# Attention in a fused block: the maximum subtracted on GpSimd, one exponential per four heads, probabilities as the stationary operand

## What is computed

```python
x = x + tanh(g_xattn[0]) * experts8(layernorm(x), gates from ctx)   # 8 experts, 2 of them used
x = x + tanh(g_ffn[0])   * swiglu4(layernorm(x), own router)        # 4 experts, 2 of them used
x = x + tanh(g_xattn[1]) * attention(layernorm(x), ctx, ctx, mask)  # 16 heads of 8 features
x = x + tanh(g_ffn[1])   * fp4_mlp(layernorm(x))                    # operands rounded to 4 bits in blocks of 16

# attention, for each batch and head
scores = q @ k.T / sqrt(8); scores = where(mask == 0, -1e9, scores)
attn = softmax(scores) @ v                 # then the heads side by side, @ Wo.T + bo
```

## Time and profile before

| | us |
|---|---|
| median of the runs | 1567.44 |
| span of the profiled execution | 1567.5 |
| PE busy | 1337.5 (85%) |
| DVE busy | 1011.9 (65%) |
| ACT busy | 872.6 (56%) |
| POOL busy | 716.2 (46%) |

### The profile page before, as it was taken

The page is one execution under the profiler, slowest core; times in us unless marked ns, Lnnn a source line. Parts: engine busy times, 40 slices in busy tenths (PEclk is TensorE's granted clock), DMA queues, the critical chain, the costliest instruction groups (busy, mean ns, idle before and its releaser), DMA issues.

```text
span 1567.5 us, 25069 instructions
## 1 busy us (share of the span) xinstructions
PE 1337.5 (85%) x6350; PEld 979.1 (62%) x6350; DVE 1011.9 (65%) x2377; ACT 872.6 (56%) x2421; POOL 716.2 (46%) x971
## 2 busy tenths in 40 slices
PE   7778988889978898879888899888998898896884
PEld 5556766667656766557666676666666576574552
DVE  6866675856668476766758566585666857574442
ACT  5535764556744575447655466455664477553652
POOL 3533554435534355444634355344553446442342
PEclk9979997999989899999989899799997999996765
DMA  3310000000000000000000000000000000000000
GB/s 99 108 41 4 5 9 15 4 6 7 5 14 4 7 8 6 16 6 8 4 20 2 9 4 10 14 4 8 8 6 14 5 9 5 6 3 7 4 4 4
DMA packets 34084, 20.48 MB, mean 13 GB/s; under 512 B 3624, under 2 KB 31888, under 8 KB 33936
## 3 DMA queue, kind: packets, MB, share of 16 engines
q1 hardware_dynamic: 33936, 18.81, 4.2%
HBM read 16.70 MB, written 2.10 MB: 12 GB/s over the span
## 4 chain that ended last, share of the span: by engine, by line
PE 45%; DVE 20%; issue 15%; POOL 10%; ACT 8%; DVEq 1%; POOLq 0%; SPq 0%; DMA 0%; ACTq 0%
PE M L1034 5%; PE U L1051 5%; PE U L877 4%; DVE h_lo L743 4%; PE U L881 4%; PE U L878 4%; PE Y L877 3%; ACT big L648 3%; PE Y L881 3%; PE M L1021 3%; DVE h L739 3%; PE Y L878 2%; PE M L1041 2%; PE M L1065 2%; POOL big L549 2%
## 5 line engine op out<-in xcount | busy, mean ns | idle before, releaser
L743 DVE TENSOR_TENSOR h_lo<-h,h_hi 128x512 fp32r<-128x512 f32 x384 | 316.9, 828 | 72.6 <-POOL h_hi L508 60.0
L508 POOL TENSOR_SCALAR h_hi<-h 128x512 fp32r<-128x512 f32 x256 | 180.5, 707 | 257.7 <-ACT h L609 230.0
L648 ACT ACTIVATE big<-big,nmax 128x128 f32<-128x128 f32 x512 | 199.8, 395 | 88.8 <-DVE nmax L841 88.3
L609 ACT ACTIVATE h<-U,biasT 128x512 f32<-128x512 f32 x256 | 175.9, 687 | 102.5 <-PE U L881 88.9
L549 POOL TENSOR_TENSOR big<-big,rinv 128x512 f32<-128x512 f32 x128 | 150.3, 1174 | 151.7 <-DVE rinv L844 151.7
L1051 PE MATMUL U<-big,Vr 128*128 128x512 f32 x256 | 150.9, 674 | 24.0 <-ACT big L653 24.0
L1034 PEld LDWEIGHTS M<-kT,qT 8*128 8x128 f32 x944 | 116.1, 189 | 84.3 <-issue 69.6
L1034 PE MATMUL M<-kT,qT 8*128 8x128 f32 x944 | 138.7, 286 | 2.2 <-ACT sg L666 2.1
L877 PE MATMUL U<-xn_hi,w_hi 128*128 128x512 f32 x256 | 119.3, 466 | 21.9 <-DVE h L739 12.9
L844 DVE RECIPROCAL rinv<-rsum 128x4 f32<-128x4 f32 x128 | 22.7, 177 | 174.4 <-ACT big L648 174.4
L619 ACT ACTIVATE h_hi<-h 128x512 fp32r<-128x512 f32 x128 | 80.9, 632 | 84.6 <-DVE h L739 81.7
(11 more groups left out here) (210 smaller groups left out, 3023.9 us busy)
## 6 DMA issues: line engine op xcount, KB each, us to landing
big<-in_L_xattn_W SPq DMA_DIRECT2D x16, 256.0 KB, 3.0
big<-in_L_ffn_w SPq DMA_DIRECT2D x12, 256.0 KB, 2.8
xin<-in_x SPq DMA_DIRECT2D x8, 256.0 KB, 2.7
nat<-in_ctx SPq DMA_DIRECT2D x8, 256.0 KB, 3.2
ctx<-in_ctx SPq DMA_DIRECT2D x32, 64.0 KB, 1.8
mask_sb<-in_mask_BxSxS_if SPq DMA_DIRECT2D x32, 64.0 KB, 1.9
out_dram<-xatt SPq DMA_DIRECT2D x32, 64.0 KB, 1.6
big<-in_L_ffn_w_down SPq DMA_DIRECT2D x1, 176.0 KB
```

The source lines that it names most:

```text
L508: nc.gpsimd.tensor_scalar(h_hi[i % 4][:, :], h32[i % 3][:, :], 1.0, 0.0, ALU.mult, ALU.add).then_inc(hi_done, 1)
L609: nc.scalar.activation(h32[i % 3][:, :], U[i % 2][:, :], ACT.Relu, bias=biasT[:, i:i + 1]).then_inc(relu_done, 1)
L648: done = nc.scalar.activation(p, p, ACT.Exp, bias=nmax[:, u % 2, r:r + 1], accum_out=rsum[:, u % 2, r:r + 1])
L743: nc.vector.tensor_tensor(h_lo[i % 4][:, :], h32[i % 3][:, :], h_hi[i % 4][:, :].bitcast(fp32), ALU.subtract).then_inc(lo_done, 1)
```

## The change

Attention's softmax is put together in another way.

- `exp`: POOL now adds `nmax` to all 512 columns of `pr` first, and ACT then takes one exponential of 512 columns, without a bias and without sums.
- The step `rsum` is gone, with its reciprocal on DVE and its multiplication on POOL.
- `Vr` is now 16 heads of 8 columns and a ninth that holds ones. `pv` is four matmuls of 9 moving columns, each with one head's transposed probabilities as the stationary operand. The result has the queries on the partitions, and the ninth column is the sum of the row. Nothing is accumulated over units.
- `ot` is on DVE: the reciprocal of the 16 sums, and one multiplication from PSUM into `On`.
- A new step `a_ot`: PE transposes `On`, ACT copies it to `OT` in one piece. It takes its turn in the M banks.

```diff
@@ -30,12 +30,12 @@
 NUDGE = 1.0 - 2.0 ** -22
-N_M = TG * 18
+N_M = TG * 19
...
 Z_SETUP, M_SETUP = 1, 4
-CHAIN0, CHAINP, CHAIN1 = 3, 3, 52
+CHAIN0, CHAINP, CHAIN1 = 3, 3, 56
@@ -114,17 +114,17 @@
 LN_STEPS = {"a_ln", "f_ln"}
-M_STEPS = {"a_cx", "a_q", "a_k", "a_v", "s", "pt", "wo", "f_xt", "f_g", "f_u", "f_ht", "f_dn"}
+M_STEPS = {"a_cx", "a_q", "a_k", "a_v", "s", "pt", "a_ot", "wo", "f_xt", "f_g", "f_u", "f_ht", "f_dn"}
...
 AT = {"start": 8, "period": 14, "a_ln": -3, "a_lnx": -1, "a_cx": 0, "a_q": 1, "a_k": 2, "cap": 2, "a_v": 8,
-      "s": (4, 7, 11, 14), "exp": (1, 1, 2, 2), "rsum": 2, "pt": 5, "pv": 7, "ot": 21, "wo": 25,
+      "s": (4, 7, 11, 14), "exp": 2, "pt": 5, "pv": 7, "ot": 21, "a_ot": 22, "wo": 25,
...
 AT_LAST = {"start": 4, "period": 12, "a_ln": -2, "a_lnx": -1, "a_cx": 0, "a_q": 3, "a_k": 1, "cap": 4, "a_v": 10,
-      "s": (5, 8, 11, 15), "exp": (1, 1, 2, 3), "rsum": 3, "pt": 5, "pv": 7, "ot": 22, "wo": 24,
+      "s": (5, 8, 11, 15), "exp": 2, "pt": 5, "pv": 7, "ot": 22, "a_ot": 23, "wo": 24,
@@ -138,14 +138,12 @@
         t = where["start"] + where["period"] * j
-        for what in ("a_ln", "a_lnx", "a_cx", "a_q", "a_k", "a_v", "cap", "ot", "wo"):
+        for what in ("a_ln", "a_lnx", "a_cx", "a_q", "a_k", "a_v", "cap", "ot", "a_ot", "wo"):
...
             put(t + first, "s", u)
-            for h, later in enumerate(where["exp"]):
-                put(t + first + later, "exp", u * HB + h)
-            for what in ("rsum", "pt", "pv"):
+            for what in ("exp", "pt", "pv"):
@@ -253,11 +251,12 @@
         kT = [sb(f"kT{i}", [P, HB * P]) for i in range(2)]
-        Vr = sb("Vr", [P, HB, P])
+        Vr = sb("Vr", [P, H, DK + 1])
...
         pr, pT = [big[:, 0, :], big[:, 1, :]], [big[:, 2, :], big[:, 3, :]]
-        nmax, rsum, rinv = (sb(n, [P, 2, HB]) for n in ("nmax", "rsum", "rinv"))
+        nmax = sb("nmax", [P, 2, HB])
+        rinv, On = sb("rinv", [P, H]), sb("On", [P, P])
@@ -283,7 +282,7 @@
         Y = [ex.enter_context(nc.psum_tensor(f"Y{i}", [P, NT], fp32)) for i in range(2)]
-        OA = U[2]
+        OA = U[2][:, 0:H * (DK + 1)].rearrange("p (h d) -> p h d", d=DK + 1)
@@ -307,7 +306,7 @@
         cap_made, oa_full, oa_emptied = sem("cap_made"), sem("oa_full"), sem("oa_emptied")
-        nmax_done, exp_done, rsum_done, norm_done = sem("nmax_done"), sem("exp_done"), sem("rsum_done"), sem("norm_done")
+        nmax_done, shifted, exp_done = sem("nmax_done"), sem("shifted"), sem("exp_done")
@@ -542,11 +541,11 @@
                         nc.gpsimd.tensor_tensor(rstd1[:, :], ve1[:, :], minus_half[:, 0:1], ALU.pow).then_inc(rstd1_done, 1)
-                    elif what == "rsum":
-
-                        pool.wait_ge(rsum_done, g1 * H + (i + 1))
+                    elif what == "exp":
+
+                        pool.wait_ge(nmax_done, g1 * H + (i + 1))
                         p = pr[i % 2].rearrange("p (h k) -> p h k", h=HB)
-                        nc.gpsimd.tensor_tensor(p, p, rinv[:, i % 2, :].unsqueeze(2).broadcast_to([P, HB, S]), ALU.mult).then_inc(norm_done, 1)
+                        nc.gpsimd.tensor_tensor(p, p, nmax[:, i % 2, :].unsqueeze(2).broadcast_to([P, HB, S]), ALU.add).then_inc(shifted, 1)
@@ -641,23 +640,14 @@
                     elif what == "exp":
-                        u, r = i // HB, i % HB
-                        if r == 0:
-                            act.wait_ge(nmax_done, g1 * H + (u + 1))
-                        p = pr[u % 2][:, r * S:(r + 1) * S]
-                        done = nc.scalar.activation(p, p, ACT.Exp, bias=nmax[:, u % 2, r:r + 1], accum_out=rsum[:, u % 2, r:r + 1])
-                        if r == HB - 1:
-                            done.then_inc(exp_done, 1)
+                        act.wait_ge(shifted, g1 * H + (i + 1))
+                        nc.scalar.activation(pr[i % 2], pr[i % 2], ACT.Exp).then_inc(exp_done, 1)
...
                         nc.scalar.activation(pT[i % 2], bank[:, :], ACT.Copy).then_inc(emptied, 1)
-                    elif what == "ot":
-
-                        act.wait_ge(oa_full, g1 * TG + (i + 1))
-                        for q in range(HB):
-                            rows = slice(32 * q, 32 * q + 32)
-                            done = nc.scalar.activation(OT[rows, :], OA[rows, q * P:(q + 1) * P], ACT.Copy)
-                        done.then_inc(oa_emptied, 1)
+                    elif what == "a_ot":
+                        bank, emptied = m_use(step)
+                        nc.scalar.activation(OT[:, :], bank[:, 0:P], ACT.Copy).then_inc(emptied, 1)
@@ -696,8 +686,9 @@
             setup, _ = chain(dve, setup_step, 0)
-            for dst in (WqT, WkT, Vr):
+            for dst in (WqT, WkT):
                 nc.vector.memset(dst[:, :, :], 0.0)
+            nc.vector.memset(Vr[:, :, DK:DK + 1], 1.0)
@@ -829,9 +820,8 @@
-                        at_r = bass.AP(Vr, 0, [Vr[:, :, :].ap[0], [P + DK, HB], [HB * DK, HB], [1, DK]])
-                        src, bias = (v.rearrange("p (q r d) -> p r q d", q=HB, r=HB) for v in (bank[:, 0:P], bv_bc[:, :]))
-                        nc.vector.tensor_tensor(at_r, src, bias, ALU.add).then_inc(emptied, 1)
+                        src, bias = (v.rearrange("p (h d) -> p h d", h=H) for v in (bank[:, 0:P], bv_bc[:, :]))
+                        nc.vector.tensor_tensor(Vr[:, :, 0:DK], src, bias, ALU.add).then_inc(emptied, 1)
@@ -839,9 +829,11 @@
                         nc.vector.tensor_reduce(nmax[:, i % 2, :], p, AX.X, ALU.max, negate=True).then_inc(nmax_done, 1)
-                    elif what == "rsum":
-                        dve.wait_ge(exp_done, g1 * H + (i + 1))
-                        nc.vector.reciprocal(rinv[:, i % 2, :], rsum[:, i % 2, :]).then_inc(rsum_done, 1)
+                    elif what == "ot":
+                        dve.wait_ge(oa_full, g1 * TG + (i + 1))
+                        link1(nc.vector.reciprocal(rinv[:, :], OA[:, :, DK]))
+                        nc.vector.tensor_tensor(On[:, :].rearrange("p (h d) -> p h d", d=DK), OA[:, :, 0:DK],
+                                                rinv[:, :].unsqueeze(2).broadcast_to([P, H, DK]), ALU.mult).then_inc(oa_emptied, 1)
@@ -1035,7 +1027,7 @@
                         bank = m_use(step)
-                        pe.wait_ge(norm_done, g1 * H + (i + 1))
+                        pe.wait_ge(exp_done, g1 * H + (i + 1))
@@ -1048,12 +1040,17 @@
                         m_made(step, ("pt", i), ("a_v", j))
-                        ins = nc.tensor.matmul(OA[:, :], Vr[:, r, :], pT[i % 2], start=(r == 0), stop=(r == HB - 1))
+                        for h in range(HB):
+                            ins = nc.tensor.matmul(OA[:, h * HB + r, :], pT[i % 2][:, h * P:(h + 1) * P], Vr[:, h * HB + r, :], start=True, stop=True)
...
                             ins.then_inc(oa_full, 1)
+                    elif what == "a_ot":
+                        bank = m_use(step)
+                        pe.wait_ge(oa_emptied, g1 * TG + (i + 1))
+                        nc.tensor.transpose(bank[:, 0:P], On[:, :], ident[:, :]).then_inc(m_full, 1)
...
                         bank = m_use(step)
-                        pe.wait_ge(oa_emptied, g1 * TG + (i + 1))
+                        m_made(step, ("a_ot", i))
```

## The result

The changed kernel takes 1663.84 us (median of 4 executions, 1661.52 to 1667.11) against 1567.18 us before. The ratio is 1.0604, with an interval of 1.0567 to 1.0641: 97 us slower, where 34.5 us faster was forecast. The profiled execution spans 1665.0 us at a mean granted clock of 0.854; before it was 0.921.

The account below looks back on a forecast made before the run. PE's own work (busy 85% of the span) was taken as the largest part, with some latency behind other engines. Terms 17 + 10 + 6 - 3.5 - 4 + 9 = 34.5 us off 1567.5 gave 1533 us, range 1505 to 1562.

Parts of the forecast that it names:

- The exponentials: On ACT: one activation at 0.62 us replaces four taking 1.66, freeing 128 us of ACT, worth nothing by itself.
- the unit's chain: Attention's softmax per unit: maximum, POOL 1.17 us, exponential 0.62, transposes; claimed 1.3 us shorter than before.
- PE's waits before the junction, +10: PE waiting for the scores' bank and for pT: half of 21 us saved, 10 us, ends 0 and 20.
- The junction, +17: Where layer and attention paths meet at xnT: 2.4 us earlier, seven times, 17 us gained, ends 0 and 32.
- `pv` on PE, +6: Probabilities-times-values on PE: eight thin passes at 0.81 us a unit instead of 0.86, 6 us gained.
- `a_ot`, -3.5 and -4: New step on PE: 32 transposes lose 3.5 us; waiting for DVE and the shifted bank turn lose 4.
- The last walk, +9: Final stage, attention alone: shorter waits for POOL's multiplication and the exponentials save 9 of 140 us, ends 2 and 20.
- The clock: Rival: thin pv passes leave the last walk at half clock, up to 29 us more, total 1562; chance 0.10.
- The argument against it: Against the clock rival: pv keeps PE occupied as long as before, and the gaps get shorter.
- The slower rival, exposed weight loads: Rival in pv: stationary loads do not overlap, slower from 0.135 us a pass, 1583 us at 0.15; chance 0.09.
- the 0.82 for faster: Chance given to the whole kernel getting faster: 0.62 + 0.12 + 0.08; same 0.08, slower 0.10.

Follow-up runs that it names:

- split_order: The change with POOL's subtraction as its own step and ACT's exponential one half slot later; 1616.2 us, ratio 1.0301 to the kernel before.
- window128: split_order with each pv pass streaming 128 moving columns in place of 9, whole attention kept; 1558.8 us, ratio 0.9943 to the kernel before.
- softmax_only: The kernel before with the new softmax alone, pv still wide, division by the sums left out; 1620.1 us, ratio 1.0340.
- the probe: PE-only program, not a kernel variant: gapless stretches of single forms and mixtures; clock 0.50 for narrow passes and scores, 1.00 for wide passes and transposes.
- pv_only: The kernel before with the new pv, ot and a_ot alone, old exponentials and POOL's multiplication kept; 1611.8 us, ratio 1.0290.

## Why the prediction was wrong

By its own steps:

- **The exponentials**: right as a price (0.63 for 0.62). This is the step that failed first: "By itself this is worth nothing, since ACT is 56% busy; it counts only where PE waits." It puts a new wait of ACT at nothing. I costed what ACT no longer does and not what it now waits for. The instruction that I listed as one link of the unit's chain, POOL's 1.17 us ahead of the exponential, stands on ACT's list too: ACT must wait for it, with `h`, `cxT`, `kT` and the MLP's copies behind. split_order shows 48 us for it, 26 of them as idle time of PE and the rest by the clock. The diff showed it: the ACT branch of `exp` waits for `shifted`, and both engines had the step in the same half slot. Before, the engine that stood behind the slow partner was DVE (174 us), and I only asked what its release was worth.
- **PE's waits before the junction, +10**: the sign is wrong. The waits I meant to halve did shrink (for `pT` from 24.0 to 11.3 us; the 14.9 us for the bank that DVE gives back late are no longer among the change's), and four of 57.4 us came, 3.1 before. The ends I gave, 0 to 20, left out a loss without a row that excluded one.
- **The junction, +17**: right in kind, a little smaller. The timeline of one of them:

```profile
863.15 0.74 DVE L758 SCALAR_TENSOR_TENSOR x<-Z,tg,xin 128x512 f32<-128x512 f32 x1
...
863.93 0.87 DVE L766 BATCH_NORM_STATS2 bn<-x 128x6 f32<-128x128 f32 x4
...
868.74 1.09 PE L988 MATMUL Z<-ident,nat 128*128 128x128 f32 x4
```

  The statistics start 0.78 us behind `x1` and `xnT` 5.59; before it was 2.38 and 7.36. So the statistics come 1.6 us earlier as forecast, and `xnT` 1.8 (1.5 to 2.5 was given). The first product behind it, with the 0.3 for ACT that made up the 2.4, comes 1.9 us earlier: 7.52 us behind `x1` (870.67) for 9.46 (817.94 behind 808.48). At 1.9 seven junctions give 13 us for the 17, if all are like this one. `pv` took 1.88 us there, its price at half.
- **`pv` on PE, +6**: the price at full clock is right, 0.80 us for eight passes against 0.81; the wrong step is that this price, at full clock, was the whole term. The row did not say what a kernel full of such passes does to the clock. At half a unit takes 1.51 to 1.88 us, and what stands around it takes up to twice as long (scores 2.00 us for 1.08, transposes 1.04 for 0.59). From split_order to window128, where only the passes get wider, this is 57 us.
- **`a_ot`, -3.5 and -4**: small as forecast; one transpose takes 0.11 us on the chain, and PE waited for `On` 2.4 us in total.
- **The last walk, +9**: part of it was there (softmax_only, with the clock at 0.69, is 5 us shorter than before, and window128 6), and in the change the clock took it: 118 us of PE's work where 98.8 stood, 153 us where 131 was forecast.
- **The rivals.** The clock's mechanism was right, and its size and chance were not. I let it act in the last walk alone (29 us, 0.10), since there PE's gaps were; the probe shows that it needs no gap, and of pv_only's loss 32 us are in the seven walks (1315 for 1283) and 8 in the last. The argument against it, that `pv` keeps PE occupied as long as before, is the one that fell. The rule of the Trainium skill that I quoted for this rival (TensorE: Matmul & The Clock Gate, Why this matters for your kernels) speaks of breaks and of padding; without breaks the clock fell all the same, and padding to 128 columns brought it back (0.941 in window128). The slower rival, exposed weight loads, did not happen: a unit takes 0.80 us, not the 1.08 at which that rival begins. Its threshold took the scores' 0.135 for a pitch, which the probe shows at 0.112. So the kernel was slower by two mechanisms, of which the order had no place in my cases, and the 0.82 for faster was too high.

In sum: from the change to window128 the order gives back 48 us and the form of the passes 57. What is left is 8 us of gain where 34.5 was forecast. The missing 26 are, as an estimate, 12 for the dearer units of `pv` in window128, 4 of the junctions, 3 of the last walk, and most of the 10 for PE's waits: window128 still waits 15.2 us for `cxT`. So the terms that I worked out from rows were a little too high, but they did not fail; what failed is that two costs were put at nothing, the place of ACT's wait in its list and the clock in the seven walks, and the two make each other worse.

## What to carry to other kernels

When work moves from one engine to another ahead of a third, look at the third's list: the price of a new wait is what is queued behind it, not the length of the link, and a place one slot later may be all that is needed. About half of that price came by the clock here, so it doesn't show as idle time of PE. A float32 matmul with few moving columns can be as cheap as its row says, and still a stretch full of them can run at half the clock, with all that stands between them; ask of each form not only its pitch but at which granted clock stretches of it run, in gapless stretches too. Where the clock is the bound, wider passes that compute what nobody needs can be faster than narrow ones.

## What was not expected of the hardware

- TensorE at 1.2 GHz while busy without a gap: most of the 240 narrow and of the 200 score passes of the probe (0.50 in the windows above), against 2.4 GHz in 200 transposes of 128x128 float32 in a row. I had taken idle time for the only cause.
- With a new 128x128 float32 stationary operand for each pass, eight passes take 0.80 us with 9 moving columns and 0.89 with 128. So 128 columns are nearly free beside 9. The score passes, with 8 rows and 128 columns, begin as far apart as the narrow ones, 0.112 us; the 1.08 us of eight of them holds what a group costs at its ends.
- A kernel gained 57 us by streaming 14 times the columns in 1024 passes.
